# One ScalarE check instruction for two chunks, with ring buffers freed in pairs and four steps reordered

## What is computed

```python
# layer 0
deg = clip(sum(adj, 1) + 1, 1)
h   = concat([x, (adj @ x + x) / deg]) @ W0 + b0
out = relu(h); out = out / max(norm(out), 1e-12)
x   = layernorm(x + out)
# layer 1
neigh = adj @ x / (sum(adj, 1) + 1)
x   = layernorm(x + concat([x, neigh]) @ W1.T)
```

## Time and profile before

| | us |
|---|---|
| median of 3 runs | 753.95 |
| lowest and highest | 752.53 to 753.97 |
| the profiled run, its own time | 753.86 |
| its span on the core | 751.7 |
| TensorE matmul busy | 632.5 (84%) |
| VectorE busy | 670.9 (89%) |
| ScalarE busy | 618.5 (82%) |
| GpSimd busy | 250.9 (33%) |
| bytes moved | 274.54 MB, 365 GB/s over the span |

### The profile page before, as it was taken

How to read it: one execution, slowest core, us unless ns; L and a number is a source line. 1 busy time by engine, 2 the same in 40 slices (tenths; PEclk the granted TensorE clock), 3 DMA queues, 4 the chain that set the end, 5 groups by cost and what they waited for, 6 DMA issues and landing times.

```text
span 751.7 us, 27897 instructions
## 1 busy us (share of the span) xinstructions
PE 632.5 (84%) x11125; PEld 579.6 (77%) x11125; DVE 670.9 (89%) x2469; ACT 618.5 (82%) x969; POOL 250.9 (33%) x344
## 2 busy tenths in 40 slices
PE   1467667778787888889899998999999999999995
PEld 0467666667676777778798887999898998989995
DVE  6879899889998998998999998999999999987894
ACT  6788898989998989899899988898998989870143
POOL 0122434333322233324335232535352434321034
PEclk9986988989999999999999999999999999999998
DMA  9999999999999999999999999999999999910002
GB/s 343 420 419 420 421 419 421 418 420 419 419 420 419 401 422 416 410 418 395 420 400 422 417 419 381 407 412 411 413 393 419 396 421 418 415 76 3 2 28 94
DMA packets 41515, 274.54 MB, mean 365 GB/s; under 512 B 4454, under 2 KB 8614, under 8 KB 8614
## 3 DMA queue, kind: packets, MB, share of 16 engines
q1 hardware_dynamic: 41152, 272.65, 88.7%
q10 hardware_dynamic: 230, 0.07, 0.0%
HBM read 270.60 MB, written 2.10 MB: 363 GB/s over the span
## 4 chain that ended last, share of the span: by engine, by line
PE 33%; DMA 23%; DVE 16%; issue 11%; ACT 10%; POOL 4%; SPq 1%; ACTq 0%; DVEq 0%; POOLq 0%
DMA a_in<-in_adj 23%; PE s_ps L388 16%; ACT junk L591 7%; PE u_ps L407 5%; DVE t_sb L812 5%; DVE e L805 4%; POOL small L1177 4%; DVE q_sb L876 2%; PE p_ps L374 2%; DVE y_sb L870 2%; PE s_ps L473 2%; PE u_ps L469 1%; PE z_ps L457 1%; PE p_ps L469 1%; SPq L339 1%
## 5 line engine op out<-in xcount | busy, mean ns | idle before, releaser
L591 ACT ACTIVATE junk<-a_in 128x2048 uint8<-128x2048 uint16 x256 | 488.6, 1912 | 17.7 <-DMA a_in<-in_adj 16.9
L388 PE MATMUL s_ps<-xh,t_sb 128*128 128x129 f16 x4096 | 389.4, 252 | 43.1 <-DVE t_sb L812 39.7
L388 PEld LDWEIGHTS s_ps<-xh,t_sb 128*128 128x128 fp8e4 x4096 | 314.3, 103 | 73.1 <-DVE t_sb L812 44.9
L805 DVE TENSOR_SCALAR e<-a_in 128x2048 uint8<-128x2048 f32 x256 | 312.0, 1225 | 24.4 <-DMA a_in<-in_adj 23.5
L1204 POOL COPY store<-pk 128x32 uint32<-128x32 uint32 (+1 forms) x250 | 151.5, 648 | 285.7 <-ACT pk L600 285.7
L812 DVE TENSOR_SCALAR t_sb<-pk 128x128 uint32<-128x128 uint32 x1024 | 156.3, 224 | 7.3 <-ACT pk L600 6.4
L374 PE MATMUL p_ps<-pow_h,e 128*128 128x16 f16 x2048 | 90.9, 171 | 66.2 <-DVE e L805 65.4
L374 PEld LDWEIGHTS p_ps<-pow_h,e 128*128 128x128 f16 x2048 | 77.8, 99 | 80.7 <-DVE e L805 68.4
L1177 POOL TENSOR_TENSOR small<-small,minus_half 128x4 f32<-128x4 f32 x32 | 70.3, 2196 | 167.9 <-DVE small L862 124.1
L407 PE MATMUL u_ps<-xh,u_sb 128*128 128x64 f16 x2976 | 105.1, 192 | 0.0
L407 PEld LDWEIGHTS u_ps<-xh,u_sb 128*128 128x128 fp8e4 x2976 | 100.1, 97 | 1.2
(11 more groups left out here) (120 smaller groups left out, 467.1 us busy)
## 6 DMA issues: line engine op xcount, KB each, us to landing
a_in<-in_adj SPq DMA_DIRECT2D x256, 1024.0 KB, 11.9
xl<-in_x SPq DMA_DIRECT2D x4, 512.0 KB, 12.8
out_h<-e SPq DMA_DIRECT2D x8, 256.0 KB, 2.5
b_sb<-in_L_gnn_b ACTq DMA_DIRECT2D x3, 0.2 KB
w_sb<-in_L_gnn_W ACTq DMA_DIRECT2D x1, 32.0 KB
w_raw<-in_L_gnn_W ACTq DMA_DIRECT2D x1, 32.0 KB
```

What stands on the lines that cost most here:

```text
L388: last = nc.tensor.matmul(s_ps[:, n % 2, at:GW], t_sb[:, b // 2, b % 2::2], xh[:, b, at:GW], start=(b == 0), stop=False)
L591: nc.scalar.activation(junk[:, t % 2, :], halves[t % R], ACT.Copy, scale=1.0 / 128, accum_out=half_sum[:, n, c:c + 1]).then_inc(s_half, 1)
L805: nc.vector.tensor_scalar(e8[:, c, :], a_in[:, t % R, :], 1.0, float(CODE), ALU.is_equal, ALU.add).then_inc(s_e, 1)
```

## The change

ScalarE sums two chunks with one instruction of 4096 values per partition instead of one of 2048 for each. `half_sum` then holds two sums a block, and SP may reuse a ring slot when the pair that the old chunk belongs to is done. take_z, take_packed(n - 1, 1), normalise and take_g stand at other places between the sums. On TensorE the cat transposes stand ahead of the pack matmuls of chunk 3. On VectorE `low_part` and `begin_acc` move from the end of block k = 3 to behind the first compare of the next block. In the tail, two waits of TensorE move, and the last add and its eight squares are done in two halves.

```diff
@@ SP
                     if t >= R:
                         sp.wait_ge(s_e, t - R + 1)
-                        sp.wait_ge(s_half, t - R + 1)
+                        sp.wait_ge(s_half, (t - R) // 2 + 1)
@@ TensorE, tail_sums, main loop and tail
+                    if j == LAST and r == TG // 2 - 1:
+                        last.then_inc(s_vps, 1)
                 last.then_inc(s_vps, 1)
...
-                    pack_chunk(n, c)
                     if e >= 0 and (k, c) == (1, 3):
                         transpose_cat(e)
+                    pack_chunk(n, c)
...
-            pe.wait_ge(s_agg, NB)
             pe.wait_ge(s_uadd, NB - START[1])
             tail_sums(0)
             transpose_cat(e)
+            pe.wait_ge(s_pk, NB * 2)
             tail_sums(1)
             dense(e)
+            pe.wait_ge(s_agg, NB)
             tail_sums(2)
@@ ScalarE
+            def sum_codes(n, pair):
+
+                t = n * NC + 2 * pair
+                for chunk in (t, t + 1):
+                    act.wait_ge(s_in[chunk % R], 16 * (chunk // R + 1))
+                if t:
+                    act.wait_ge(s_half, t // 2)
+                nc.scalar.activation(junk[:, :], halves[t % R // 2], ACT.Copy, scale=1.0 / 128,
+                                     accum_out=half_sum[:, n, pair:pair + 1]).then_inc(s_half, 1)
...
-                sum_codes(n, 0)
                 if e >= 0 and k == 2:
                     take_z(e)
+                if n:
+                    take_packed(n - 1, 1)
+                sum_codes(n, 0)
                 if e >= 0 and k == 3:
                     normalise(e)
-                sum_codes(n, 1)
-                if n:
-                    take_packed(n - 1, 1)
                 if n >= 2:
                     take_sums(n - 2)
                 if e >= 0 and k == 3:
                     take_h(e)
-                sum_codes(n, 2)
                 take_packed(n, 0)
+                sum_codes(n, 1)
                 if e >= 0 and k == 3:
                     take_g(e)
-                sum_codes(n, 3)
                 if e >= 0 and k == 1:
                     take_cat(e)
@@ VectorE, main loop
                 compare(n, 0)
+                if e >= 1 and k == 0:
+                    low_part(e - 1)
+                    begin_acc(e - 1)
                 if n:
                     unpack(n - 1, 0)
...
-                if e >= 0 and k == 3:
-                    low_part(e)
-                    begin_acc(e)
@@ VectorE, tail
+            def add_last(h):
+
+                dve.wait_ge(s_vps, LAST + h + 1)
+                dve.wait_ge(s_vadd, LAST)
+                rows = acc[:, NB - TG + h * BR:NB - TG + (h + 1) * BR, :]
+                link(nc.vector.tensor_tensor(rows, v_ps[LAST % 3][:, h * BR:(h + 1) * BR, 0:F], rows, ALU.add))
...
+                if g == NV - 1:
+                    add_last(0)
                     variance(g - 1)
-                add_tail(NV + g)
-                if g == NV - 1:
+                    square_last(0)
+                    add_last(1)
+                    square_last(1)
                     last_variance()
+                else:
+                    if g:
+                        variance(g - 1)
+                    add_tail(NV + g)
```

More of the change, by code:

```diff
@@ L24 @@
 CB = CH // P
+NK = NC // 2
 R = 6
@@ L45 @@
 TG = 8
+LAST = 2 * NB // TG - 1
 NV = NB // TG
@@ L144, in gnn_kernel @@
         half_sum = sb("half_sum", [P, NB, NC], F32)
-        junk = sb("junk", [P, 2, CH], U8)
+        pair_sum = half_sum[:, :, 0:NK]
+        junk = sb("junk", [P, 2 * CH], U8)
         dcol = sb("dcol", [P, NB], F32)
@@ L580, in _ @@
             nc.scalar.copy(warm[:, :], ident[:, 0:1])
[L582 to L592, removed]
+            halves = [a_in[:, i:i + 2, :].rearrange("p c i -> p (c i)").bitcast(U16).rearrange(
+                "p (b two) -> p b two", two=2)[:, :, 1] for i in range(0, R, 2)]
+            def sum_codes(n, pair):
[6 more added lines that the diff above has]
+                                     accum_out=half_sum[:, n, pair:pair + 1]).then_inc(s_half, 1)
             def take_packed(n, h):
@@ L937, in add_tail, with square_last @@
                 ins.then_inc(s_vadd, 1)
+            def add_last(h):
[3 more added lines that the diff above has]
+                link(nc.vector.tensor_tensor(rows, v_ps[LAST % 3][:, h * BR:(h + 1) * BR, 0:F], rows, ALU.add))
+            def square_last(h):
+                dve.wait_ge(s_fvar, NV - 4)
+                for n in range(NB - TG + h * BR, NB - TG + (h + 1) * BR):
+                    ins = nc.vector.scalar_tensor_tensor(out=sqf[:, (NV - 1) % 4, n % TG, :], in0=acc[:, n, :], scalar=1.0,
+                                                         in1=acc[:, n, :], op0=ALU.mult, op1=ALU.mult,
+                                                         accum_out=fvar[:, 1, n:n + 1])
+                link(ins)
             def variance(g):
@@ L948, in last_variance @@
                 rows = slice(NB - TG, NB)
[L949 to L955, removed]
                 nc.vector.scalar_tensor_tensor(out=fvar[:, 1, rows], in0=fvar[:, 1, rows], scalar=1.0 / F,
@@ L968, in verdict @@
             def verdict():
-                dve.wait_ge(s_half, NB * NC)
+                dve.wait_ge(s_half, NB * NK)
                 tmp = u_sb[:, :, :].rearrange("p b i -> p (b i)").bitcast(F32)
-                r_hs, sums, want = tmp[:, 0:NB * NC], tmp[:, NB * NC:NB * NC + NB], tmp[:, NB * NC + NB:NB * NC + 2 * NB]
-                link(nc.vector.tensor_scalar(r_hs, hs_flat, ROUND, None, ALU.add))
+                r_hs = tmp[:, 0:NB * NK].rearrange("p (n c) -> p n c", c=NK)
+                sums, want = tmp[:, NB * NC:NB * NC + NB], tmp[:, NB * NC + NB:NB * NC + 2 * NB]
+                link(nc.vector.tensor_scalar(r_hs, pair_sum, ROUND, None, ALU.add))
                 link(nc.vector.tensor_scalar(r_hs, r_hs, ROUND, None, ALU.subtract))
-                link(nc.vector.tensor_tensor(r_hs, r_hs, hs_flat, ALU.not_equal))
-                link(nc.vector.tensor_reduce(bad[:, 0:1], r_hs, AX_X, ALU.max))
-                link(nc.vector.tensor_reduce(sums, half_sum[:, :, :], AX_X, ALU.add))
+                link(nc.vector.tensor_tensor(r_hs, r_hs, pair_sum, ALU.not_equal))
+                link(nc.vector.tensor_reduce(bad[:, 0:1], tmp[:, 0:NB * NK], AX_X, ALU.max))
+                link(nc.vector.tensor_reduce(sums, pair_sum, AX_X, ALU.add))
                 link(nc.vector.tensor_scalar(want, dcol[:, :], 1.0 / CS, -1.0, ALU.mult, ALU.add))
@@ L1064, in _ @@
             for g in range(NV):
-                if g:
+                if g == NV - 1:
+                    add_last(0)
                     variance(g - 1)
-                add_tail(NV + g)
-                if g == NV - 1:
+                    square_last(0)
+                    add_last(1)
+                    square_last(1)
                     last_variance()
+                else:
+                    if g:
+                        variance(g - 1)
+                    add_tail(NV + g)
                 if g >= 2:
```

## The result

The changed kernel takes **772.22 us** in the median (771.45 to 773.47), the kernel before, run beside it, 753.24 (752.10 to 753.97): a ratio of 1.0256, 95% interval 1.0244 to 1.0269. It is slower by 2.6%. The profiled execution took 772.12 us with a span of 770.0. The forecast was 777.4, range 757 to 784: the sign and the mechanism are right, and the sum is 5.2 us too high.

The account below looks back on a forecast made before the run. Landings and TensorE were both taken to be at their limit, so a longer ring through ScalarE costs time. Span 751.7 + 12.5 (ring) + 12.4 (clock) - 0.47 - 0.90 (tail) = 775.2, plus 2.16 around it: 777.4 us, range 757 to 784.

Parts of the forecast that it names:

- The ring: Cat transposes, dense product, ScalarE's list to normalise, h transposes: 17.1 us instead of 14.7 per late group, +12.5 us in all.
- The clock: TensorE at half speed after each 3.1 us rest: 1.55 us for each of eight h transposes, +12.4 us; other end zero.
- The first h transpose behind the landings: Where loads stop setting the pace, h transposes come at 377.5 us; no delay from the change up to there.
- The seven stretches in between: TensorE's own work from h transposes to the next cat transposes, seven late groups: 178.86 us of busy time.
- The tail: End of the kernel: one wait gone, -0.47 us, and half the last add and four squares hidden, -0.90 us.
- Freeing by pairs: Ring slots released an instruction later: taken as zero; other end 0.3 us for each of 16 groups, 5 us.
- Rival 2: No stall, but pair freeing lets the load queue run dry: 757.5 us, chance 7%.
- the move of low_part: VectorE may wait for take_g, unpack behind it; TensorE's work hides that: zero, or up to 1 us a group.
- Rival 5: VectorE's wait for take_g reaches TensorE, 1 us or more in seven groups, longer clock fall: 785 to 795, chance 5%.
- Rival 1: TensorE's stall comes as computed but the clock does not fall: 765.0 us, chance 22%.
- Rival 3: ScalarE's ring no longer than TensorE's 14.0 us, three pairs under 7.7 us: faster, 748.9 us, chance 8%.
- Rival 4: Nothing measurable, the tail's gain against a little loss: 753 to 755 us, chance 3%.

Follow-up runs that it names:

- e6: Changed kernel plus one extra ScalarE copy of 1024 values between take_z and normalise at block k = 2; 778.18 (profiled), 786.63, 790.20 and 794.89 us.
- e7: Changed kernel plus one extra ScalarE copy of 1024 values at the start of each block k = 0, outside the stretch from take_z to normalise; 772.13 us.
- e4_fill: Changed kernel plus 40 matmuls filling TensorE's rest ahead of the h transposes from 378.6 us on; 766.76 us, ratio 1.0186.
- e9_tail_only: Kernel before with only the change's tail edits (two moved TensorE waits, last add and its squares in halves); 752.13 us against 753.58, ratio 0.9982.
- e5_pair_free: Kernel before with one edit, ring slots reused only when both chunks of a pair are summed, single sums kept; 754.02 us against 753.16, ratio 1.0011.
- e1: Changed kernel with normalise moved back ahead of the first pair of block k = 3, all else kept; 760.86 us, ratio 1.0102.
- e8_low_late: Changed kernel with normalise ahead of the first pair of k = 3, and low_part and begin_acc behind the next block's first unpack; 757.23 us, ratio 1.0057.

## Why the prediction came out as it did

**The ring: right.** From z to `normalise` the six chunks in three instructions were priced 3.61 us each and took 3.60 to 3.61 by their pitch (the 1.91 us in the working is the mean of all sums on the page, 1912 ns; the earlier trace rows has 1.89); take_z stood at 3.05 behind the cat transposes in the sum and at 3.08 in the trace; the ring was to be 17.1 us and is 17.2 in the late groups (17.1 once). e6 and e7 show that it is this stretch that bounds. TensorE stands for 2.65 us, not 3.1, in the late groups, mostly because its wait for t_sb did not go, as the prediction had it, but fell from 0.72 to 0.26 us.

**The clock: right in kind, the mis-sized term.** The sum put 8 x 1.55 = 12.4 us on it, a fall behind every rest. In the profiled execution five of eight came: 5 x 1.55 = 7.8 us, so 4.65 us of the 5.2 are here. Four of the five lie ahead of the last h transpose of the loop, one behind it. The size of one was about right (27.4 to 27.8 us against 26.1; by e4_fill all of them together are 5.5 us, against 7.8 by this count of one execution). The failed step is "a rest of 3.1 us is longer than the one that was followed by the fall", from one row at 454 us: at 420.7, 462.1 and 594.1 the rests of 2.16, 2.40 and 2.65 us were followed by a clock of 1.00. One fall had been seen, and one rest without; that bears a chance for each group, not a certainty for eight. Nor does the size decide: the rest of 1.32 us at 378.6, the shortest of the eight, was followed by the fall.

**Smaller terms, which nearly cancel, by luck.** The first h transpose behind the landings came at 378.6, not 377.5 (+1.1). The first two rings were 18.1 and 17.9 us: seven sum to 121.9, not 120.05 (+1.85). The seven stretches in between sum to 181.7; less four falls that is 175.5, not 178.86 (-3.36). Of this, 7 x 0.2 = 1.4 are the pack matmuls, which stand ahead of the cat transposes no more and so left the long stretch; that the prediction gave nothing for them was wrong. The first two stretches account for 1.9, with 8 and 11 matmuls less than before, and this was not followed. Together 378.6 + 121.9 + 181.7 = 682.2, the last h transpose of the loop, 18.3 us later than before where 23.35 were forecast with the falls in.

**The tail.** From there to the end of the span both kernels take 87.8 us (751.7 less 663.9, 770.0 less 682.2). The prediction had +1.55 for a fall and -1.4 for the edits; both came (0.52 at 682.2; 1.4 us by e9_tail_only) and cancel.

**Costed at nothing.** Freeing by pairs was nothing in the old order (e5_pair_free). Rival 2 falls with the stall that it denies, and its 5 us for an empty queue were not seen there either. That the move of low_part is hidden held in the changed kernel, but the cover was put down to TensorE's work between the dense product and that quarter, and e1 shows a wait of 0.98 us in spite of that work, as soon as the h transposes come in time. It was hidden by the loss itself. Rival 5 had the mechanism; it waits behind the ring.

**The rivals.** Rival 1, the clock holds, gave 765.0; with the clock held by filler it is 766.8. So 772.2 lies between rival 1 and the forecast: some falls came, not all and not none. Rival 3, faster, fails by its own condition: the three pairs took 10.8 us, not under 7.7. Rival 4, nothing measurable, falls with the 19 us.

The rule of the Trainium skill (page "Perfetto Trace Analysis", section "Optimizing Scalar/DVE Operations") is that breaking up instructions may help when ScalarE isn't saturated but makes other engines wait. That is the state here: ScalarE is busy for 77% and TensorE waits for it. But the measurement goes against the remedy. Split back into two instructions in the same order the ring is longer, 17.7 us, and the kernel slower, 785.4 us (e3_split); what helps is to move other work out of the way (e1_norm_first). The prediction weighed the change by the second half of the rule and had the sign right, but by its own ring and not by that rule.

## What to carry to other kernels

Before several small instructions are merged on an engine that executes in order, write down which result leaves that engine next and who waits for it: here 22.9 us less work on ScalarE came with 19 us more time, and 11.4 of them went again when one call changed places with one merged instruction. A dose tells such a ring from other work cheaply: put the same small extra instruction once inside and once outside the suspected stretch, and compare. And a wait may be hidden only by the one that is being removed, so look at the next engine's trace again after each fix.

## What was not expected of the hardware

- Rests of TensorE of the same size were followed by different clocks. Waits for h_sb of 1.32, 2.56, 2.65, 2.65 and 2.65 us (378.6, 504.5, 549.5, 637.4, 682.2) were followed by 0.51 to 0.58 for 3.4 us, others of 2.16, 2.40 and 2.65 us by 1.00. TensorE's timeline of the kernel with the dose in the ring shows one of 3.60 us, behind which the clock was 1.00 (the stretch from 597.6 shown above):

```profile
597.61 0.63 PE L454 MATMUL c_ps<-ident,h_sb 128*64 128x128 f32 x4 [3.60 <-ACT h_sb L654]
```

  With the rest filled by 2.4 us of matmuls it was 1.00 in each of the four stretches shown. What else decides it was not found.
- The changed kernel's executions lie within 2 us of each other, those with the split pair within 7, with the dose in the ring within 17, and with the same dose and the late rests filled within 6. Long rests alone don't explain it: e8_low_late, whose late rests are short, spreads over 4.9 us.
- One sum of 4096 values takes 3.61 us and two of 2048 take 3.78, a saving of 0.17 us for each instruction merged away (pitch from start to next start).
